# Conv edge chunks of 11 and 12 columns in turn, and lot products in three tiles of two columns

## The reference

```python
def _nnconv(x, src, dst, edge_attr, ew, eb, rw, rb):
    W = (edge_attr @ ew + eb).reshape(E, 16, 16)
    xj = x[src]
    msg = jnp.einsum('ei,eio->eo', xj, W)
    return jax.ops.segment_sum(msg, dst, N) + x @ rw + rb

h = relu(layernorm(x))
h = relu(batchnorm(_nnconv(h, ..., layer 0)))
h = relu(batchnorm(_nnconv(h, ..., layer 1)))
x = x + relu(_nnconv(h, ..., layer 2)) @ pred_w + pred_b
h = relu(layernorm(x))
x = x + segment_max(h[src] * edge_weight1, dst) @ W.T + b
```

## Time and profile before

| | |
|---|---|
| median of three runs | 10234.24 us |
| the profiled execution | 10232.45 us, its span 10230.6 us |
| conv passes, steady part | about 200 to 2510, 2750 to 5090 and 5325 to 7590 us |
| max pass | about 7950 to 10030 us |
| TensorE (PE) busy | 9348.9 us, 91% |
| PE weight load (PEld) busy | 8493.2 us, 83% |
| VectorE (DVE) busy | 6967.5 us, 68% |
| ScalarE (ACT) busy | 6915.7 us, 68% |
| GpSimd (POOL) busy | 7502.7 us, 73% |

### The profile page before, as it was taken

How to read it: one execution, slowest core, us unless ns; L and a number is a source line. 1 busy time by engine, 2 the same in 40 slices (tenths; PEclk the granted TensorE clock), 3 DMA queues, 4 the chain that set the end, 5 groups by cost and what they waited for, 6 DMA issues and landing times.

```text
span 10230.6 us, 159899 instructions
## 1 busy us (share of the span) xinstructions
PE 9348.9 (91%) x49036; PEld 8493.2 (83%) x49036; DVE 6967.5 (68%) x10638; ACT 6915.7 (68%) x6857; POOL 7502.7 (73%) x7820
## 2 busy tenths in 40 slices
PE   6999999998599999999849999999993999999994
PEld 4888888887388888888738888888883999999994
DVE  7777777777387878787737787878782544444442
ACT  3777777775377777777627777777763887777772
POOL 6777777777577777777747777777775777777776
PEclk9999999999699999999969999999996999999996
DMA  4333333333233333333323333333331211111121
GB/s 114 94 97 97 97 93 97 97 97 81 59 97 98 93 98 96 97 93 97 89 54 93 97 97 97 93 98 96 98 87 22 45 40 40 40 40 40 40 42 20
DMA packets 373818, 808.28 MB, mean 79 GB/s; under 512 B 151096, under 2 KB 211601, under 8 KB 373528
## 3 DMA queue, kind: packets, MB, share of 16 engines
q0 software_dynamic: 250112, 432.57, 20.5%
q1 hardware_dynamic: 123671, 375.30, 11.6%
HBM read 676.39 MB, written 130.92 MB: 79 GB/s over the span
## 4 chain that ended last, share of the span: by engine, by line
PE 50%; issue 17%; POOL 16%; ACT 13%; DVE 2%; DMA 1%; ACTq 0%; POOLq 0%; DVEq 0%; SPq 0%
PE pY L730 41%; POOL gathered L555 16%; PE pY L752 7%; ACT hot_key L615 6%; ACT apart L610 6%; PE pY L472 2%; DMA gathered<-max_table,idx 1%; ACT xeT L801 1%; PE pT L740 0%; ACTq L242 0%; DVE msg L949 0%; PE pT L461 0%; DVE tmp L278 0%; DVE rank L1060 0%; DVE carry_hi L278 0%
## 5 line engine op out<-in xcount | busy, mean ns | idle before, releaser
L730 PEld LDWEIGHTS pY<-part,hot_key 128*128 128x128 f32 x44640 | 8031.1, 188 | 584.2 <-issue 460.2
L730 PE MATMUL pY<-part,hot_key 128*128 128x400 f32 x44640 | 8446.7, 348 | 55.0 <-DVE xe L867 24.2
L555 POOL DMA_INDIRECT gathered<-conv_table,idx x5580 | 5341.8, 957 | 1885.1 <-issue 1593.4
L867 DVE TENSOR_REDUCE xe<-pY 128x16 f32<-128x400 f32 x5580 | 3127.7, 568 | 1416.2 <-PE pY L730 1407.4
L610 ACT ACTIVATE apart<-key_pair,zone_lane 128x1408 f16<-128x1408 f16 (+1 forms) x1984 | 2859.2, 1488 | 1203.2 <-PE pY L730 974.7
L615 ACT ACTIVATE hot_key<-apart,hot_line 128x1408 fp32r<-128x1408 f16 (+1 forms) x1984 | 3048.4, 1584 | 33.2
L555 POOL DMA_INDIRECT gathered<-max_table,idx x1736 | 1670.3, 962 | 601.4 <-issue 536.9
L949 DVE TENSOR_REDUCE msg<-gathered 128x240 f32<-128x2160 f32 x744 | 1558.6, 2095 | 0.2
L278 DVE TENSOR_TENSOR gathered<-pY,pe_attr 128x432 f32<-128x432 f32 x1488 | 775.8, 563 | 633.1 <-PE pY L752 632.8
L801 ACT COPY xeT<-pT 112x128 f32<-112x128 f32 x744 | 188.8, 254 | 1223.5 <-PE pT L740 1223.5
L752 PE MATMUL pY<-edge_w,xeT 48*128 48x432 f32 (+1 forms) x2976 | 736.5, 544 | 143.1 <-ACT xeT L801 143.1
(11 more groups left out here) (133 smaller groups left out, 1621.8 us busy)
## 6 DMA issues: line engine op xcount, KB each, us to landing
key_pair<-key_rows SPq DMA_DIRECT2D x248, 672.0 KB
scanned<-run_pair SPq DMA_DIRECT2D x248, 416.0 KB, 2.5
gathered<-conv_table,idx POOLq DMA_INDIRECT x5580
attr_pair<-in_attr SPq DMA_DIRECT2D x186, 208.0 KB, 2.5
gathered<-max_table,idx POOLq DMA_INDIRECT x1736
key_pair<-key_rows SPq DMA_DIRECT2D x248, 78.0 KB
conv_table<-gathered SPq DMA_DIRECT2D x36, 360.0 KB, 2.3
conv_table<-rows SPq DMA_DIRECT2D x24, 360.0 KB, 2.3
```

The lines of the kernel that those rows point to most:

```text
L555: e.indirect_dma_start(out=G[s][:, t, 0:width], out_offset=None, in_=table[:, :], in_offset=bass.IndirectOffsetOnAxis(ap=idx[s][:, t:t + 1 ...
L730: ins = e.matmul(pG[bank], hot_key[s][:, z, at:at + P], part[:, z * NEAR:(z + 1) * NEAR, :], start=(z == 0 and k == 0), stop=(z == ZONES - ...
L867: e.tensor_reduce(xe[s][:, at:at + D], pG[j % BANKS].rearrange("p (r d) -> p d r", d=D), AX.X, ALU.max).then_inc(s_pick.sem, 1)
```

## The change

In the conv passes the number of TensorE's columns becomes a pair, `TP_CONV = (11, 12)`: 11 in slot 0 and 12 in slot 1, so POOL gathers 15 and 14 columns in turn. The one-hot matrices of slot 1 become 12 * 128 = 1536 wide. The max pass keeps 12 and 12. The counts on semaphores (`picked`, `since_bank`) follow.

A lot (6 and 5, or 6 and 6 columns) is now three pieces of up to two columns: matmuls over 32 rows at partitions 0, 32 and 64, 288 columns wide. The third goes to columns 128 to 415 of the bank that also takes the transposes (`pT[0]`). The wait for DVE's multiply of the lot before therefore moves from the product to the transpose. The product of lot 0 stands one column later, and so does DVE's `lot_product` of it.

```diff
-TP_CONV, TP_MAX = 11, 12
-TH = -(-TP_CONV // 2)
-LOTS = ((0, TH), (TH, TP_CONV))
-TRIO = 3
-PIECES = [[(k, min(TRIO, b - a - k)) for k in range(0, b - a, TRIO)] for a, b in LOTS]
-HALF = 64
-DEEP = TRIO * D
-LOT = HALF + DEEP
+TP_CONV, TP_MAX = (11, 12), (12, 12)
+TH = 6
+LOTS = [((0, TH), (TH, tp)) for tp in TP_CONV]
+PAIR = 2
+PIECES = [[[(k, min(PAIR, b - a - k)) for k in range(0, b - a, PAIR)] for a, b in lots] for lots in LOTS]
+TILES = 3
+DEEP = PAIR * D
+LOT = TILES * DEEP
...
-        pE = pY[0]
+        pE = [pY[0][:, 0, 0:PAIR * ROW], pY[0][:, 1, 0:PAIR * ROW], pT[0][:, P:P + PAIR * ROW]]
...
-            cols = slice((TP_KEYS - tp) * P, PE_EDGES)
+            cols = slice((TP_KEYS - tp[s]) * P, PE_EDGES)
...
-                a, b = LOTS[half]
-                gate(e, "pe", s_pick, number(c) * tp + (b + b_pick))
+                a, b = LOTS[c[1]][half]
+                gate(e, "pe", s_pick, picked(c) + (b + b_pick))
+
+                gate(e, "pe", s_multiplied, number(c) * 2 + (half + b_mul))
...
-                gate(e, "pe", s_multiplied, number(c) * 2 + (half + b_mul))
-                for q, (k, m) in enumerate(PIECES[half]):
-                    rows_of = slice(q * HALF, q * HALF + DEEP)
-                    e.matmul(pE[:, q, 0:m * ROW], xeT[rows_of, :], edge_w[rows_of, 0:m * ROW],
+                for q, (k, m) in enumerate(PIECES[c[1]][half]):
+                    rows_of = slice(q * DEEP, (q + 1) * DEEP)
+                    e.matmul(pE[q][:, 0:m * ROW], xeT[rows_of, :], edge_w[rows_of, 0:m * ROW],
...
                 pe_turn(e, c1, 0)
-                pe_step(e, c1, HEAD + 5)
+                for j in range(HEAD + 5, HEAD + 7):
+                    pe_step(e, c1, j)
                 pe_product(e, c1, 0)
-                for j in range(HEAD + 6, tp):
+                for j in range(HEAD + 7, tp[c1[1]]):
                     pe_step(e, c1, j)
...
-                next_picks(7, 8)
+                next_picks(7, 8, 9)
                 if not is_max and c1 is not None:
                     lot_product(e, c1, 0)
-                next_picks(*range(9, tp))
+                next_picks(*range(10, tp[1 - s]))
```

More of the change, by code:

```diff
@@ L30 @@
 PER_BANK = 512 // CW
-TP_CONV, TP_MAX = 11, 12
-TP_KEYS = max(TP_CONV, TP_MAX)
-TH = -(-TP_CONV // 2)
-LOTS = ((0, TH), (TH, TP_CONV))
-TRIO = 3
-PIECES = [[(k, min(TRIO, b - a - k)) for k in range(0, b - a, TRIO)] for a, b in LOTS]
-HALF = 64
-DEEP = TRIO * D
-LOT = HALF + DEEP
+TP_CONV, TP_MAX = (11, 12), (12, 12)
+TP_KEYS = max(TP_CONV + TP_MAX)
+TH = 6
[5 more added lines that the diff above has]
+LOT = TILES * DEEP
 BANKS = 4
@@ L55 @@
 assert CHUNKS % SLOTS == 0 and CHUNKS <= P and LANES * NB == N and DIGITS == 3 and NEAR <= 2 * ZONES * ZONES
-assert TH <= 2 * TRIO and LOT <= P and TP_MAX * D <= 2 * LOT and TP_CONV >= HEAD + 6 and PE_EDGES <= NB * D
+assert all(len(p) == TILES for lots in PIECES for p in lots) and TH == PAIR * TILES and LOT + PAIR * ROW <= 512 and TP_KEYS * D <= 2 * LOT and min(TP_CONV) >= HEAD + 7 and PE_EDGES <= NB * D
 assert W0 * W1 * W2 == EPAD and LOOKS * LOOK == NB and W0 <= P and GB * (W1 + 1) <= 512
@@ L553, in pool @@
                         gate(e, "pool", s_idx[s], i + (b_idx[s] + 1))
-                        for t in range(steps):
+                        for t in range(steps[s]):
                             e.indirect_dma_start(
@@ L578, in node_gather @@
             on("scalar")(act)
-            got = pool_gather(name, table, width, GB, iters, ready)
+            got = pool_gather(name, table, width, [GB] * SLOTS, iters, ready)
             def vec_pair(e, i, last):
@@ L658, in edges @@
             tp = TP_MAX if is_max else TP_CONV
-            tg = T - tp
+            tg = [T - k for k in tp]
             iters = CHUNKS // SLOTS
@@ L677, in number, with picked @@
                 return c[0] * SLOTS + c[1]
+            def picked(c):
+                return c[0] * sum(tp) + sum(tp[0:c[1]])
             pair = SLOTS * T * attr_width
@@ L713, in edges, with since_bank @@
             bump(s_tab)
-            def since_bank(j):
+            def since_bank(s, j):
                 if j >= BANKS:
                     return BANKS
-                return tp + j - max(k for k in range(tp) if k % BANKS == j)
+                before = tp[1 - s]
+                return before + j - max(k for k in range(before) if k % BANKS == j)
             def pe_step(e, c, j):
@@ L724, in pe_step @@
                 bank = j % BANKS
-                at = (TP_KEYS - tp + j) * P
-                gate(e, "pe", s_pick, number(c) * tp + (b_pick + j - since_bank(j) + 1))
+                at = (TP_KEYS - tp[s] + j) * P
+                gate(e, "pe", s_pick, picked(c) + (b_pick + j - since_bank(s, j) + 1))
                 for z in range(ZONES):
@@ L813, in act_factors @@
                     gate(e, "act", s_multiplied, number(c) * 2 + (b_mul - 1))
-                    e.copy(pe_attr[s][:, :, 0:EF], attr[s][:, tg:T, :]).then_inc(s_pe_factors.sem, 1)
+                    e.copy(pe_attr[s][:, 0:tp[s], 0:EF], attr[s][:, tg[s]:T, :]).then_inc(s_pe_factors.sem, 1)
                     gate(e, "act", s_multiplied, number(c) * 2 + b_mul)
-                    e.copy(pA[:, 0:tg * EF], attr[s][:, 0:tg, :].rearrange("p t f -> p (t f)")
+                    e.copy(pA[:, 0:tg[s] * EF], attr[s][:, 0:tg[s], :].rearrange("p t f -> p (t f)")
                            ).then_inc(s_factors.sem, 1)
@@ L861, in pick @@
                 i, s = c
-                gate(e, "dve", s_gath, number(c) * tp + (b_gath + j + 1))
+                gate(e, "dve", s_gath, picked(c) + (b_gath + j + 1))
                 at = j * D
-                if not is_max:
-                    half, k = divmod(j, TH)
-                    at = half * LOT + k // TRIO * HALF + k % TRIO * D
                 e.tensor_reduce(xe[s][:, at:at + D], pG[j % BANKS].rearrange("p (r d) -> p d r", d=D),
@@ L876, in lot_product @@
                     gate(e, "dve", s_pe_factors, number(c) + (b_pefac + 1))
-                gate(e, "dve", s_prod, number(c) * 4 + (2 * half + 2 + b_prod))
+                gate(e, "dve", s_prod, number(c) * (2 * TILES) + (TILES * half + TILES + b_prod))
                 g4 = G[s][:, :, :].rearrange("p t (d f) -> p t d f", f=FB)
[L880 to L883, removed]
+                for q, (k, m) in enumerate(PIECES[c[1]][half]):
+                    at = LOTS[s][half][0] + k
+                    ins = tt(e, g4[:, tg[s] + at:tg[s] + at + m, :, :],
+                             pE[q][:, 0:m * ROW].rearrange("p (t d f) -> p t d f", d=D, f=FB),
                              pe_attr[s][:, at:at + m, :].unsqueeze(2).to_broadcast([P, m, D, FB]), ALU.mult)
@@ L891, in body @@
                 g = G[s]
+                near, far = tg[s], tp[s]
                 def mark(ins):
@@ L902, in next_picks @@
                     for j in js:
-                        if c1 is not None and j < tp:
+                        if c1 is not None and j < tp[1 - s]:
                             pick(e, c1, j)
@@ L935, in body @@
                     next_picks(3, 4)
-                    gate(e, "dve", s_pick, n * tp + (tp + b_pick))
-                    m_p = mark(tt(e, rows_of(tg, T), xe[s][:, 0:tp * D].rearrange("p (t d) -> p t d", d=D),
-                                  by[:, tg:T, :], ALU.mult))
+                    gate(e, "dve", s_pick, picked(c) + (far + b_pick))
+                    m_p = mark(tt(e, rows_of(near, T), xe[s][:, 0:far * D].rearrange("p (t d) -> p t d", d=D),
+                                  by[:, near:T, :], ALU.mult))
                     next_picks(5)
@@ L998, in vec @@
                 indices(e, (0, 1))
-                for j in range(tp):
+                for j in range(tp[0]):
                     pick(e, (0, 0), j)
-                    if j == 8 and not is_max:
+                    if j == 9 and not is_max:
                         lot_product(e, first, 0)
@@ L1018, in edges @@
             for cc in (s_gath, s_pick):
-                bump(cc, CHUNKS * tp)
+                bump(cc, iters * sum(tp))
             if not is_max:
@@ L1432 @@
         conv_w.append(diagonal(GB, block, CW, bias))
-        trio = diagonal(TRIO, block[:, :ROW], ROW, bias[:ROW])[:-1]
-        edge_w.append(np.concatenate([trio, np.zeros((HALF - DEEP, TRIO * ROW), np.float32), trio]))
+        edge_w.append(np.tile(diagonal(PAIR, block[:, :ROW], ROW, bias[:ROW])[:-1], (TILES, 1)))
     lin_w = np.stack([diagonal(GB, f["L0_gnn_pred_w"], D, f["L0_gnn_pred_b"]),
```

26 lines of the change are left out of this document (13 added, 13 removed).

## The result

The changed kernel takes 10410.03 us (median of four runs, 10407.92 to 10412.33) against 10234.83 us for the kernel before, a ratio of 1.0171 with a 95% interval of 1.0153 to 1.0189: 175 us slower. The forecast was 10346 us, slower by 112. Direction and mechanism held, and one term was much too small.

The account below looks back on a forecast made before the run. A loop of TensorE and ACT was taken to bound the kernel, POOL following. Slot 1 at 20.31, slot 0 at 18.06 and +0.13 for keys gave 38.50 us a pair, +112 us: 10346 us, range 10275 to 10455.

Parts of the forecast that it names:

- The bound: Conv passes: TensorE and ACT form one loop of 37.90 us a pair; POOL is full but only follows.
- The rival in which POOL sets the pace: Conv passes: POOL's gathers bound the kernel, so a pair takes 37.52 us, 10163 us in all, faster; chance 7%.
- The twelfth column and the wider matrices: Slot 1: one more TensorE column, +1.45 us a pair, and four longer ACT activations in the loop, +0.43.
- The wait left in slot 1: TensorE's wait for ACT's copy, once a pair, forecast at 0.42 + 0.43 = 0.85 us.
- Three tiles: Conv products: narrower records with a free third tile make each 0.24 us shorter, -0.96 a pair.
- The rival in which the third is not free: Conv products: a third tile in turn costs 0.48 us a product, 1.92 a pair, 10703 us; chance 12%.
- what I worked out from the 3.07 times: Conv products: an estimate that 0.48 us of streaming would become 0.62.
- The later product: Slot 0: product of lot 0 behind the eleventh column ends the wait for ACT, chunk 18.06 us; slot 1 gains nothing.
- The keys: Slot 0: the key load, issued after slot 1's `hots_end`, comes late for ACT; +0.13 us a pair.
- my upper bound of 0.4: Slot 0: the most the late key load was taken to cost, 0.4 us a pair, +50 us in the range.
- DVE, POOL and the moved wait at nothing: Conv passes: DVE's extra 1.5 us a pair, one gather less and transposes waiting for DVE's multiply cost nothing.
- The range: Whole kernel: 10275 to 10455 us around the forecast, with upward room for late keys or a costlier third tile.

Follow-up runs that it names:

- width: The kernel before, with only slot 1's one-hot matrices made 1536 instead of 1408 elements wide; 10316.30 us, ratio 1.0081.
- eleven: The changed kernel with 11 columns in both slots of the conv passes, keeping three tiles and the later product; 10159.88 us, ratio 0.9930.
- keys_order: The `keys` kernel, with the product of lot 0 behind the last column in both slots; 10168.67 us, ratio 0.9937.
- keys: The changed kernel, with each slot's keys loaded by themselves once that slot's one-hot matrices are through; 10306.75 us, ratio 1.0072.
- keys_back: The `keys` kernel, with the product of lot 0 put back behind one column, as in the kernel before; 10377.46 us, ratio 1.0138.
- two_inputs: The `eleven` kernel plus one unused DVE product of two SBUF tensors in each conv chunk; 10215.90 us.
- one_input: The `eleven` kernel plus one unused DVE reduction over one SBUF tensor in each conv chunk; 10158.33 us.

## Why the prediction was right, and where it was not

**The bound.** TensorE and ACT as one loop, POOL following: right for the kernel before. `width` lengthens nothing but ACT's part and the time follows by 83 us. The rival in which POOL sets the pace is out, since TensorE still waits for ACT in slot 1 (0.68 us) and POOL idles. It was a close second, though: `eleven` shows POOL's own pace as 18.73 us, 0.22 under the 18.95 of the kernel before.

**The twelfth column and the wider matrices, +1.45 and +0.43.** Slot 1 was forecast at 20.31 us and takes 20.24. The column alone shows in `keys_order`, where TensorE waits for nothing: slot 1 takes 19.49 us and slot 0 18.03, a difference of 1.46. `width` gives 0.42 for the 0.43 by its chunks, 0.45 by the medians. The wait left in slot 1 is 0.68 us, and I had 0.85: I had added ACT's 0.43 to the 0.42 of the earlier trace rows, which is the wait of slot 0. In slot 1 the kernel before waits 0.35:

```profile
1227.84 0.98 PE L752 MATMUL pY<-edge_w,xeT 48*128 48x432 f32 x4 [0.35 <-ACT xeT L801]
```

**Three tiles, -0.24 a product.** Right: 0.69 us, all tiles side by side. The rival in which the third is not free is out, and with it what I worked out from the 3.07 times of the Trainium skill (TensorE: Matmul & The Clock Gate, Part 3, Packing small matmuls). The same section gives a span of one matmul and some 4 ns for each further tile; with that rule the trace agrees, its records of three tiles start 7 ns apart.

**The later product.** Right: slot 0 on TensorE alone was forecast at 18.06 us, and `keys`, where nothing else holds it, takes 18.05. `keys_back` shows that the move is worth 0.39 us.

**The keys, +0.13.** This is the step that failed, by its size. The mechanism was in the forecast: `hots_end` of slot 1 later, the eleventh column of slot 0 sooner, the keys between them. But measured it costs 18.65 - 18.05 = 0.60 us a pair, beyond my upper bound of 0.4, and 103 us by the medians where I had put 24 (over all three passes slot 0 takes 18.61 us, so 0.56 a pair). The chain of slot 0 gives the sum: the load is issued 6.42 us after the product of lot 1 starts (forecast 6.35), its keys are used 6.1 us later (5.41), and ACT needs another 6.1 us; together 18.6, with no TensorE in it. So nearly all of the miss is the time from issue to use. I took one row of the max pass. It was a short one, the mean of the 47 such waits there is 5.5, and in the conv pass, for a cause that stays open, it is 6.1. Each tenth of a us beyond the cover is 19 us. I had seen that the transfer would be more crowded, and priced it at a fifth of what it took. The other terms add up: 112 - 24 + 103 is 191, less 0.07 a pair in slot 1, 178, against 175 measured.

**DVE, POOL and the moved wait at nothing.** Right for all. `keys_order` has the new wait at the transposes too, and TensorE has no gap there. POOL's idle time appeared as said: its 74 waits for indices, 116.4 us, are 1.8 us a pair beyond the 0.30 that stands before every gather.

**The range.** It held the result, near its upper end (10455), and that is luck. With my upper bound for the keys alone it would have ended at 10346 + 50 = 10396, under the 10410 measured; the rest of the room was there for a third tile that costs, which did not happen.

The change fails as it stands since two waits eat what it frees. With both of them removed (`keys_order`) it is 64 us faster than the kernel before, with all three parts of the change in use. The smaller change, `eleven`, gets 73 us by leaving the twelfth column away: the tiles and the later product take TensorE's own work to 18.05 us, as slot 0 of `keys` shows, and POOL then paces at 18.73. The two are within 9 us of each other, one bound by TensorE at 37.52 us a pair, the other by POOL at 37.46.

## What to carry to other kernels

Where an engine is busy 98% of the time, ask first for whom it waits in the other 2%: here the 0.4 us a chunk told of a loop through a second engine, and work added to either side of it counted in full. When a change shortens one side of a loop, look for the next thing that was in time only because that side was slow, such as a load that is issued at the end of the last use; its slack is worth measuring in the same traffic, not in a quieter stage. And order matters as much as amount: the same product, moved from before the column that ACT waits for to behind it, where it covers a wait, gave 0.39 us in slot 0 (`keys_back` against `keys`) and 0.76 in slot 1 (`keys` against `keys_order`).

## What the runs showed of the hardware that I had not expected

A gather's 0.94 us on POOL is not a constant. In the kernel before, between 400 and 2400 us, 103 of 1584 gathers take 1.16 us in the mean, one a chunk, and every one of them starts 0.6 us after DVE's scan does and ends 1.8 us after it. The scan (1.01 us) reads two SBUF tensors. In `keys_order` the gather starts 0.2 us into the scan, ends at the same 1.8 us, and takes 1.60 us. So a gather that starts within the scan ends 0.8 us after the scan does, wherever in it it began. Gathers that are already running when the scan starts are not lengthened (106 of them in the kernel before, none over 0.95 us). `two_inputs` and `one_input` show that it goes by the operands: two SBUF inputs hold a gather, one input for the same time holds none. The two differ in what they write as well, 1024 elements against 64, but that is not it: in the kernel before 208 gathers start inside DVE's multiply of the gathered columns, which writes 1920 elements to SBUF and reads one of its two inputs from PSUM, and none of them takes over 0.96 us.

The Trainium skill (SBUF — State Buffer, SBUF: two separate sides) says that DVE and GpSimd share a port pair as an exclusive lock, taken by a DVE operation with two SBUF inputs against a GpSimd operation that reads SBUF; with that rule the trace agrees for the gathers, down to the one-input case. It also says that a GpSimd operation that started first blocks DVE for as long as it runs, and that does not show here: the scan takes 1.01 us where a gather is running at its start (the kernel before) and 1.02 where none is (`keys_order`).

In a loop that another engine paces this costs nothing, as in the kernel before, but it hides POOL's room. In `width` a chunk is 0.21 us longer than in the kernel before and POOL still shows no idle time: its long gather has gone from 1.16 to 1.38 us in the mean and fills the difference. An engine without idle time need not be the bound. In `eleven`, which POOL paces, the gathers fell into a phase in which only 2 of 1602 are long, and the 0.2 us a chunk that I had counted as POOL's own were not there. That is why it came out 55 us faster than I expected.
